# Four interleaved step streams of a hybrid convolution, attention and Fourier kernel: empty steps of the norms taken out, and the order strings of all engines written anew

## The reference, cut to what matters

```
x = x + conv0(x)              # per image: mean over pixels -> 4 routing weights (sigmoid);
x = x + conv1(x)              # 1x1 to 96 channels, relu, 3x3 depthwise, relu, 1x1 back to 24
t = tokens(x)                 # 3136 tokens of 24 channels per image
t = t + linear_attention(layernorm(t))
t = t + ffn0(layernorm(t))    # 24 -> 96 -> 24, rounded to fp8 and fp16 on the way
t = t + fourier(layernorm(t)) # 24 -> 48, FFT over the 3136 tokens, complex diagonal mix, relu,
                              # inverse FFT, 48 -> 24
t = t + ffn1(layernorm(t))
```

## Time and profile before

| | |
|---|---|
| median of 3 runs | 2623.15 us (2612.80 to 2631.39) |
| profiled execution | 2623.52 us |
| its span, first to last instruction | 2621.4 us |
| mean granted clock of TensorE | 0.874 of full |
| busy: PE, DVE, ACT, POOL | 2183.9, 1927.7, 1611.5, 113.7 us |
| DMA | 29.69 MB, 5.0% of the 16 engines' time |

### The profile page before, as it was taken

How to read it: one execution, slowest core, us unless ns; L and a number is a source line. 1 busy time by engine, 2 the same in 40 slices (tenths; PEclk the granted TensorE clock), 3 DMA queues, 4 the chain that set the end, 5 groups by cost and what they waited for, 6 DMA issues and landing times.

```text
span 2621.4 us, 49010 instructions
## 1 busy us (share of the span) xinstructions
PE 2183.9 (83%) x19776; PEld 1269.9 (48%) x19776; DVE 1927.7 (74%) x3744; ACT 1611.5 (61%) x2758; POOL 113.7 (4%) x290
## 2 busy tenths in 40 slices
PE   3677878998889888998889887998889988986865
PEld 1233334663446534664446534465346634662653
DVE  4886987897768795799858795885957988456153
ACT  3344457855677575765777565864867647757554
POOL 1000000000000000000000000000000000000000
PEclk9887989998789898999889896996889988976665
DMA  5001001000020001000010002000010000000000
GB/s 137 1 1 19 1 1 20 2 2 1 1 38 2 1 1 35 4 2 1 4 35 2 2 1 38 1 2 1 1 30 2 2 1 1 20 2 1 20 1 19
DMA packets 108592, 29.69 MB, mean 11 GB/s; under 512 B 104144, under 2 KB 104272, under 8 KB 107984
## 3 DMA queue, kind: packets, MB, share of 16 engines
q1 hardware_dynamic: 108368, 26.56, 5.0%
HBM read 16.91 MB, written 9.63 MB: 10 GB/s over the span
## 4 chain that ended last, share of the span: by engine, by line
DVE 41%; PE 38%; ACT 11%; issue 6%; SPq 3%; DMA 1%; ACTq 0%; DVEq 0%
DVE acc L1475 20%; PE P L745 6%; PE P L726 5%; PE P L945 4%; PE P L1037 3%; SPq L586 3%; DVE SQ L1621 3%; PE P L794 3%; PE P L958 2%; PE P L986 2%; DVE arena L1605 2%; DVE T L1491 2%; PE P L767 1%; DVE T L1635 1%; PE P L1000 1%
## 5 line engine op out<-in xcount | busy, mean ns | idle before, releaser
L1475 DVE SCALAR_TENSOR_TENSOR acc<-H,Dm,acc 128x784 f32<-128x784 f32 x1024 | 989.4, 1027 | 74.1 <-ACT acc L1113 73.6
L726 PE MATMUL P<-T,Wk 112*128 112x448 f32 (+1 forms) x768 | 393.5, 605 | 77.3 <-ACT H L1106 37.7
L745 PE MATMUL P<-H,diag 64*64 64x392 f32 x4608 | 404.6, 501 | 18.4 <-DVE T L1491 18.4
L1106 ACT ACTIVATE H<-P,biasA 128x448 f32<-128x448 f32 (+1 forms) x384 | 236.0, 622 | 250.5 <-PE P L726 159.9
L745 PEld LDWEIGHTS P<-H,diag 64*64 64x64 f32 x4608 | 172.2, 135 | 234.0 <-issue 203.7
L726 PEld LDWEIGHTS P<-T,Wk 112*128 112x128 f32 x768 | 131.5, 203 | 201.5 <-ACT H L1106 103.3
L1136 ACT ACTIVATE acc<-P,biasT 128x392 f32<-128x392 f32 x128 | 68.6, 584 | 185.5 <-PE P L745 185.5
L794 PE MATMUL P<-T,pack_b 112*112 112x448 f32 x224 | 125.1, 655 | 15.0 <-DVE T L1580 7.9
L1491 DVE SCALAR_TENSOR_TENSOR T<-P,bias,T 112x392 f32<-112x392 f32 x128 | 77.2, 621 | 73.0 <-PE P L767 72.7
L970 PE MATMUL P<-pack_b,arena 128*96 128x112 f32 x928 | 111.5, 269 | 22.8 <-DVE roots L1621 11.7
L1113 ACT ACTIVATE acc<-H,Dm 128x784 f32<-128x784 f32 x128 | 121.9, 952 | 13.6 <-PE P L767 11.4
(11 more groups left out here) (205 smaller groups left out, 3766.8 us busy)
## 6 DMA issues: line engine op xcount, KB each, us to landing
xin<-in_x SPq DMA_DIRECT2D x224, 42.0 KB, 2.3
out_y<-arena SPq DMA_DIRECT2D x8, 1176.0 KB, 6.0
pack_b<-in_pack_b SPq DMA_DIRECT2D x1, 3926.5 KB, 18.0
arena<-in_pack_s SPq DMA_DIRECT2D x1, 1584.0 KB, 8.8
pack_a<-in_pack_a SPq DMA_DIRECT2D x1, 1084.0 KB, 5.4
pack_i<-in_pack_i SPq DMA_DIRECT2D x1, 320.0 KB, 3.1
arena<-in_pack_k SPq DMA_DIRECT2D x1, 192.0 KB, 3.3
```

The costliest lines, as they stand in the source:

```text
L726: pe.matmul(conv_rows(slice(0, 128), HB[(NP * s + e) % len(HB)], n), Wk1[:, 128 * j:128 * (j + 1)], image_rows(T[q % 3], a, n), start=True ...
L745: last = pe.matmul(conv_rows(slice(64 * h, 64 * (h + 1)), CVB + r, HH), diag[64 * r:64 * (r + 1), tap, :], H1[64 * r:64 * (r + 1), slot(s, ...
L1106: act.activation(H1[:, slot(s, j), o:o + n, 1:1 + HW], conv_rows(slice(0, 128), HB[(NP * s + e) % len(HB)], n), ACT.Relu, bias=biasA[:, j, ...
L1475: ins = ve.scalar_tensor_tensor(a, H1[:, slot(s, j), r:r + SR, c:c + HW], Dm[:, j, tap:tap + 1], a, ALU.mult, ALU.add)
```

## The change

In `layer_norm` on PE, the norms 1 and 3 have nothing to centre, since their input has mean zero already. Their 7 centring steps held no instruction, yet each was a turn of m or b. The `yield` now stands inside the condition, so those turns no longer exist: 56 of m and 56 of b over 8 quads. No instruction is added or removed on any engine.

The four strings of `TURNS` are replaced by new ones. TensorE's goes from 2593 turns to 2481, which are all turns with instructions in them before as well; ScalarE keeps 2273 and VectorE 2073, GpSimd its 144 steps. The order inside a stream is that of the generator and does not change; only how the four streams are interleaved does.

```diff
@@ TURNS, first and last lines of each string; what lies between is replaced too
     "gpsimd": (
-        "d7 b1 c10 m1 c1 m1 c5 m1 c4 b2 c2 m2 c4 b2 c1 m1 c4 b2 m1 c1 m1 c3 b1 c1 b1 m1 c4 b2 c1 m1 c1 m1 c4 "
+        "c8 m1 c2 d1 m1 c6 m1 c4 b3 d1 c1 m1 c2 m1 c2 b1 c1 m1 b1 c3 b1 c1 b1 m1 c1 m1 c3 b1 m1 c3 b1 c1 b1 c2 "
...
     "tensor": (
-        "c8 m1 c17 d1 c4 d2 c2 d1 c2 d8 c15 d1 c4 d2 c2 m1 d1 c4 d2 m2 d1 m2 d2 m2 d1 m2 d2 m1 c3 m2 c3 m2 c1 "
...
-        "b3 m4 b3 m4 b1 m2 b2 m3 b2 m1 b176 "
+        "c15 d1 c5 m1 c1 d1 c2 d1 c5 d2 c2 d1 c2 d2 c1 d4 c8 d1 c7 d2 c1 d1 c4 m1 c1 d1 c1 d1 c1 m1 c1 m1 d2 "
...
+        "b1 m1 b6 m3 b7 m1 b141 "
     "scalar": (
-        "c6 m1 c20 d4 c8 d4 c6 d8 c17 d1 c2 d3 c4 m1 c4 d4 c3 m1 c3 m1 d4 m1 d2 m1 d2 m1 c3 m1 c3 m1 c4 m1 c2 "
+        "c8 m1 c8 d1 c6 d1 c2 d1 c1 d1 c5 d2 c2 d1 c2 d1 c3 d2 c1 d1 c2 d5 c15 d2 c1 d2 c5 d2 c4 m1 d2 c3 m1 "
...
     "vector": (
-        "m1 c27 d2 c18 d1 c1 d1 c18 d1 c1 d1 c2 d2 c23 d1 c1 d1 c18 d2 c15 d1 c1 d1 c9 d2 m1 c1 m1 c1 m2 c1 "
...
-        "b2 m2 b2 m1 b2 m1 b2 m2 b2 m2 b2 m2 b2 m1 b7 m1 b7 m8 b1 m2 b3 m2 b3 m1 b1 m4 b1 m3 b2 m1 b78 "
+        "c3 m1 c20 d1 c2 d1 c14 d1 c2 d1 c16 d1 c1 d1 c9 d2 c24 d2 c16 d1 c1 d1 c14 d2 c12 d2 m1 c1 m2 c1 m2 "
...
+        "m1 b2 m1 b1 m1 b4 m2 b1 m1 b7 m1 b3 m4 b67 "
@@ layer_norm on TensorE
                 for c in range(NCK):
-                    yield
                     if i == 0:
+                        yield
                         pe.wait_ge(written.sem, written.at(q, 2 * NS + rows_added(c) if n == 0 else c + 1))
```

More of the change, by code:

```diff
@@ L86 @@
     "gpsimd": (
-        "d7 b1 c10 m1 c1 m1 c5 m1 c4 b2 c2 m2 c4 b2 c1 m1 c4 b2 m1 c1 m1 c3 b1 c1 b1 m1 c4 b2 c1 m1 c1 m1 c4 "
-        "b2 c1 m1 c4 b2 m1 c1 m1 c4 b2 c2 m1 c3 b2 c1 m2 c4 b2 m1 c3 b1 c1 b1 m1 c2 m1 c4 b2 c1 m1 c3 b2 m3 "
-        "b5 "
[3 rows of a table added]
     ),
     "tensor": (
[46 rows of a table removed]
[47 rows of a table added]
     ),
     "scalar": (
[37 rows of a table removed]
[39 rows of a table added]
     ),
     "vector": (
[23 rows of a table removed]
[28 rows of a table added]
     ),
```

## The result

The changed kernel takes 2464.02 us (4 runs, 2458.48 to 2473.06) against 2619.17 for the kernel before on the same chip (4 runs): a ratio of 0.9406, 95% interval 0.9359 to 0.9453. The forecast was 2593 with a range from 2560. The sign was right; the gain is 155 us where I had 30.

The account below looks back on a forecast made before the run. No engine is saturated; time is lost by order, engines waiting while other streams' ready work stands behind. Gains of 24 + 10 + 1 less 5 make 30 us, off 2623.5 gives 2593 us; 8-in-10 range 2560 to 2635.

Parts of the forecast that it names:

- term 1: Quad 5's input: quad 2's store no longer stands in front of the loads; 10 us gained, bounds 5.5 and 17.9.
- Term 2: Other input transposes in the middle: PE does other steps during input DMAs; 17 us less PE idle, bounds 0 and 33.5.
- Term 3: PE's ping-pong with ACT and DVE: fewer direct pairs in ffn 0, attention output, conv hidden; 10, 17 and 4 us less idle.
- a weight of one half: Share of the 48 us of PE idle in terms 2 and 3 taken to reach the end: 24 us; bounds 0.38 and 0.88.
- the tail: Last back's order the same by necessity, last middle and quad-6 back end together ahead of it: nothing gained.
- rival D: Slower by the clock: granted share falling from 0.874 by 0.02 gives 2619 us, by 0.05 gives 2659; chance 0.08.
- Term 4: Start: setup moved behind the first router, first tap at 58.0 instead of 59.13 us; gain 1 us, bounds 0 and 7.9.
- Term 5: Quads 3 and 5: norm 2 steps on DVE ahead of a layer's first tap delay the taps; cost 5 us, bounds 0 and 20.
- rival C: Slower: DVE's taps queue behind 24 additional norm and attention steps before a layer's first tap; 2651 us, chance 0.08.
- rival E: The store still blocks the loads, quad 6's output copies standing closer to its input ones; 2603 us, chance 0.03.
- Rival B: Off the path: PE's idles go, but DVE or the next dependence takes their place; 2611 to 2620 us, chance 0.23.
- The check that I named for being wrong altogether: In the middle, the span between the routers of successive quads grows; no size given.

Follow-up runs that it names:

- experiment 8: Changed kernel with a ring of seven input groups (XG = 7) instead of four, x loads also ahead of three weight packs at the start: 2413.83 us, ratio 0.9208.
- experiment 9: Kernel before, in its own old order, with a ring of seven input groups (XG = 7) instead of four: 2574.9 us, ratio 0.9841.
- experiment 2: Kernel before without its empty turns, new order on all four engines only behind the router of quad 7's second layer: 2585.96 us, ratio 0.9878.
- experiment 6: Kernel before without its empty turns, 28 ffn additions on VectorE each moved behind the next tap: 2625.44 us, ratio 1.0014.
- Experiment 5: Kernel before without its empty turns, new order on VectorE alone in the second-layer stages of quads 3 and 4: 2659.74 us, ratio 1.0162.
- experiment 11: Kernel before without its empty turns, new order only from quad 4's second-layer router to quad 5's first-layer router: 2606.51 us, ratio 0.9957.
- experiment 7: Kernel before without its empty turns, setup_rest behind the first router (VectorE) and the sigmoid (ScalarE), dependent steps later too: 2620.53 us, ratio 0.9991.

## Why the prediction was wrong

**The step that failed is the sum.** Beside term 1 it counted as gain only 48 us of PE idle time (terms 2 and 3) times a weight of one half. It left the clock out, put the tail at nothing, and had no term for the rest of the waits in the second-layer stages. The runs showed in its place 84.1 us less idle and 73.6 us less busy PE time, 35.8 us from the tail alone, and 80.7 us in the six second-layer stages. The waits that terms 1 to 3 name fell by 39 us (6.2 at the input transposes, 21.6 at L870, 11.8 at L726, none at L910), where I had 53.5; so over half of PE's lost idle time lay in no term.

1. *The weight.* I took one half, between PE's share of the chain and its busy share in a stretch. Experiments 8 and 9 measured it on PE's input waits behind the first router: 37.2 us of span for 38.0 us of waits gone, and 47.8 for 43.2 (the others of experiment 9, in the start, were hidden by DVE's setup). It is about one, but with the clock in it: 16.9 and 29.4 us of these spans are idle time, 0.44 and 0.68 of the waits, and the rest is busy time. As the price of idle time alone one half was not far off; as the whole price it was half of what was measured. When PE's share of the chain is 38%, that says who was last, not what an idle us of PE costs. The weight is the smaller part of the miss: at one, terms 2 and 3 would give 48 instead of 24, and the sum 54 of the 155.

2. *The clock.* I priced it on the slower side only (rival D) and wrote that "time also hangs on how idle time is spread, which my sum leaves out". Busy time is 73.6 of the 157.7 us. The earlier trace rows had shown that there was clock to win: 0.94 granted in a stretch with 229.62 us busy, 0.83 in one with 228.43. They also show that the sum of idle time alone doesn't set it, since that is 32.4 and 33.6 us there. Per us of idle time removed, busy time fell by 1.2 us (20.3 / 16.9) in experiment 8 behind the first router, 0.63 (18.4 / 29.4) in 9, 1.0 in 2's tail and 0.88 in the whole change. These shares are rough, each from one profile of either kernel: the profile of experiment 6, whose time is that of the kernel before, has 14.9 us more busy PE time (2198.8 against 2183.9). The rule of the Trainium skill ("TensorE: Matmul & The Clock Gate", section "A second HAM failure mode: psum-queue depth-cycling", on idles between groups of matmuls) had made me ask for a fall alone; whether many short idles cost more than few long ones no run here shows, since long and short ones went together. Nor is it isolated which of the removed idles gave the clock back; the busy times are an account, made at the same instructions.

3. *DVE's waits.* I counted pairs on TensorE. In the second-layer stages DVE's waits shrank by 87.2 us and PE's by 32.5. Three groups (L1588, L1475, L1491), 90.4 us together there before, lost 59.4 and had no term. Experiment 5 shows that DVE's new string alone doesn't remove them, so they can't be read off that string; that the new strings gain by fitting the engines to each other is my reading of this. Which single pairing carries most of it is open: experiment 6 tried one and found nothing.

4. *The tail* I costed at nothing "by necessity". It gave 35.8 us (experiment 2). Only the last back's order is fixed; ahead of it DVE's longest wait for a norm's root (L1500) went from 29.3 to 9.5 us, and L870's waits of 6.4 us went.

*Term 1* was right in place and size, 10 forecast and 11.2 measured for its stage (experiment 11, which changes all that is new in the stage and not the store alone). Its mechanism is in the trace, but not to the letter: the store leaves just behind the first transpose, and the last three don't follow directly on out6 (the last ffn output step ahead of them) but wait 3.5 us for their DMAs. What shrank is DVE's wait at L1430. (Its working says seven steps between the last transpose and the router; the order printed there has six.) *Term 2*, 17 us of waits, was wrong: they fell by 6.2 in all, and 2.0 of that are quad 5's. The DMAs take as long (2.3 us from issue to landing in both kernels); that the transposes run sooner behind the slots that they wait for would explain it, but isn't shown. *Term 3*: L870 went as said (22.7 to 1.1); L726 lost 11.8 us where I had 4; L910 lost nothing, although its direct pairs fell from 32 to 18 of 120. So a count of pairs was good in one case of three. *Term 4* held (experiment 7: first tap at 57.64, forecast 58.0). *Term 5* and rival C have the wrong sign: L1519's waits fell from 80.8 to 56.4 though 24 more steps stand ahead of the taps, and the first five taps of quad 0 run without a break. Rival D's clock rose, rival E did not occur at quad 5. Rival B, DVE taking over, did not either: its idle time shrank by more than PE's.

The check that I named for being wrong altogether was growth between routers. I had not named its opposite, that every second-layer stage in the middle but quad 1's shrinks by 11 to 19 us.

## What to carry to other kernels

When an order is replaced as a whole, don't sum single pairs: cut the trace of before at a point that recurs, and read for each stage the idle time of both leading engines and the granted clock. A stage of 157 us in which PE is busy for 127 at 0.83 and DVE for 112, beside one of 133 us in which PE is busy for 130 at 1.00, has some 30 us of idle time and, by an estimate from the two clocks, most of a fifth of its busy time to give. That is an upper bound, of which this stage gave 18.3; my far end, a 0.88 weight on known waits, lay below the result. Price a removed wait of the engine with the most work at about one, with what the clock gives back already in it, and try the buffer depth before the order: one constant was worth 43 us in the old order and 50 in the new.

## What the runs showed that I had not expected

- With identical instructions and order, removing 53.9 us of waits for input DMAs took 20.2 us off the busy time of TensorE (mean granted clock 0.907 to 0.922).
- The stage in which PE was idle for 2.4 of 132.6 us (450.67 to 583.27) shows a granted clock of 1.00; the same stage after the change has 3.4 of 133.9 us and 0.98. The two with 30 and 33 us idle of 157 and 151 show 0.83 and 0.81. That is a tendency, not a rule: quad 0's first-layer stage has 29 us idle of 91 at 0.89, and quad 3's went from 11.6 us idle of 164.8 at 0.95 to 4.8 of 160.7 at 0.93.
- A new string on VectorE alone, in two stages of fifteen, cost 37 us, though the four new strings together gain in both.
